# Decoder block on Trainium2: expert biases fetched per tile and added by VectorE, in place of bias products on TensorE

## What is computed

```python
x = _layernorm(x + attn(x, ...))                      # with biases on Q, K, V and O
x = _layernorm(x + (ctx @ Wv) @ Wout + bout)          # what the cross-attention comes to
h  = silu(einsum('nd,edh->neh', xf, up_w) + up_b)     # 8 experts, 256 -> 256
ye = einsum('neh,ehd->ned', h, down_w) + down_b       # 256 -> 256
y  = einsum('ned,ne->nd', ye, comb)                   # best 2 of 8 experts, weights renormalised
x = _layernorm(x + y + shared(x))
```

## Time and profile before

| what | value |
|---|---|
| three runs, us | 479.09, 479.58, 479.75 (median 479.58) |
| profiled execution, us | 479.18 |
| its span, us | 477.3 |
| PE busy | 454.2 us, 95% of the span |
| DVE, ACT, POOL busy | 303.3, 288.8, 189.1 us |
| mean granted TensorE clock | 0.982 of full |

### The profile page before, as it was taken

How to read it: one execution, slowest core, us unless ns; L and a number is a source line. 1 busy time by engine, 2 the same in 40 slices (tenths; PEclk the granted TensorE clock), 3 DMA queues, 4 the chain that set the end, 5 groups by cost and what they waited for, 6 DMA issues and landing times.

```text
span 477.3 us, 11145 instructions
## 1 busy us (share of the span) xinstructions
PE 454.2 (95%) x3613; PEld 397.2 (83%) x3613; DVE 303.3 (64%) x1248; ACT 288.8 (61%) x913; POOL 189.1 (40%) x212
## 2 busy tenths in 40 slices
PE   7998999999999999999999999988999999999982
PEld 6886888988889898898988988877898889999961
DVE  3376598557695585776765769678885543333496
ACT  3686556665666567556675565865534464665556
POOL 1899297220002001211142654434512874655530
PEclk9999899999999999999999999999998999999995
DMA  5851121410010000020011213211021663343775
GB/s 166 304 173 45 60 89 45 135 45 1 1 45 2 1 13 23 24 78 1 1 46 43 83 54 117 62 45 48 33 68 57 177 171 109 113 121 113 226 256 180
DMA packets 26541, 40.28 MB, mean 84 GB/s; under 512 B 3199, under 2 KB 17555, under 8 KB 26483
## 3 DMA queue, kind: packets, MB, share of 16 engines
q1 hardware_dynamic: 21532, 27.86, 19.0%
q0 software_dynamic: 3408, 9.33, 5.4%
q10 hardware_dynamic: 1547, 2.40, 1.7%
HBM read 26.96 MB, written 12.61 MB: 83 GB/s over the span
## 4 chain that ended last, share of the span: by engine, by line
PE 83%; DVE 8%; ACT 5%; DMA 2%; issue 1%; ACTq 0%; SPq 0%; DVEq 0%
PE bank L297 18%; PE bank L298 17%; PE bank L299 17%; PE bank L813 6%; PE bank L775 6%; PE bank L786 6%; PE bank L838 3%; PE bank L953 2%; ACT probs L1114 2%; PE bank L943 2%; PE bank L967 2%; PE bank L861 1%; PE bank L728 1%; DVE xt_lo L1312 1%; DMA xacc<-in_x_t 1%
## 5 line engine op out<-in xcount | busy, mean ns | idle before, releaser
L1114 ACT ACTIVATE probs<-probs,negmax 128x128 f32<-128x128 f32 x256 | 99.7, 394 | 50.6 <-DVE negmax L1341 50.5
L297 PE MATMUL bank<-w_hi,ot_hi 128*128 (+1 forms) x284 | 83.4, 294 | 3.2 <-ACT qkv L1085 3.0
L298 PE MATMUL bank<-w_lo,ot_hi 128*128 (+1 forms) x284 | 81.1, 285 | 0.0
L299 PE MATMUL bank<-w_hi,ot_lo 128*128 (+1 forms) x284 | 80.6, 284 | 0.0
L1341 DVE CUSTOM_DVE_ANT_0 probs<-bank,mask 128x128 f32<-128x128 f32 x256 | 61.1, 284 | 14.2 <-PE bank L775 14.1
L584 POOL DMA_INDIRECT xg_dram<-xacc,place x32 | 32.1, 1005 | 92.7 <-PE bank L813 35.0
L297 PE MATMUL bank<-xt_hi,w_hi 128*128 128x512 f32 x144 | 61.4, 426 | 1.6 <-DVE w_lo L1322 0.6
L297 PEld LDWEIGHTS bank<-w_hi,ot_hi 128*128 128x128 f32 x284 | 54.3, 191 | 6.9 <-ACT qkv L1085 3.8
L1077 ACT ACTIVATE qkv<-bank,cols 128x512 f32<-128x512 f32 x64 | 42.1, 678 | 29.5 <-PE bank L299 29.5
L299 PE MATMUL bank<-xt_hi,w_lo 128*128 128x512 f32 x144 | 56.9, 395 | 0.0
L298 PE MATMUL bank<-xt_lo,w_hi 128*128 128x512 f32 x144 | 56.8, 395 | 0.0
(11 more groups left out here) (215 smaller groups left out, 1036.2 us busy)
## 6 DMA issues: line engine op xcount, KB each, us to landing
qkv<-xg_dram SPq DMA_DIRECT2D x39, 128.5 KB, 2.1
ex_raw<-in_w_experts SPq DMA_DIRECT2D x18, 256.0 KB, 2.6
w_raw<-in_w_quads SPq DMA_DIRECT2D x10, 256.0 KB, 4.7
xacc<-in_x SPq DMA_DIRECT2D x4, 512.0 KB, 3.6
ex_raw<-in_w_cross SPq DMA_DIRECT2D x4, 512.0 KB, 3.2
w_raw<-in_ctx_t_in ACTq DMA_DIRECT2D x4, 512.0 KB, 3.8
w_raw<-in_w_quads SPq DMA_DIRECT2D x3, 512.0 KB, 7.1
xacc<-in_x_t SPq DMA_DIRECT2D x3, 512.0 KB, 6.3
```

What stands on the lines that cost most here:

```text
L297: pe.matmul(o, a_hi, b_hi, start=first, stop=False)
L298: pe.matmul(o, a_hi, b_lo, start=False, stop=False)
L299: return pe.matmul(o, a_lo, b_hi, start=False, stop=last)
L1114: nc.scalar.activation(tile, tile, ACT.Exp, scale=-1.0, bias=negmax[:, s.par, h, j:j + 1], accum_out=sums[:, s.par, h, j:j + 1]).then_inc( ...
```

## The change

The two bias products of a tile go, and so do the nine expert rows of `rows` (only `bout` is left, with one column of `sel`). The down biases, with the shared one added, are written to a small DRAM tensor `down_rows`; the up biases are in `up_rows` as before. For each tile SP reads the expert's number from `list_e` and issues a DMA that copies that bias row to all 128 partitions, once for up and once for down, each into two buffers (`BR`). DVE adds the bias while it evacuates PSUM: `tile_up_bias` writes `th`, on which SiLU then works in SBUF, and `tile_y`, which was ACT's, is DVE's. ACT takes x_hi(i+2) ahead of silu(i). `load_y` of groups 0 to 2 moves from SP to ACT's queue.

```diff
@@ sync
+            def load_bias(i, into, of, landed, taken):
+                if i >= BR:
+                    sp.wait_ge(taken, i - BR + 1)
+                e = sp.value_load(list_e[0:1, i:i + 1], min_val=0, max_val=NE)
+                sp.dma_start(into[:, i % BR, :], of[bass.ds(e, 1), :].rearrange("o n -> (o n)").partition_broadcast(P)
+                             ).then_inc(landed[i % BR], 16)
+            sp.wait_ge(in_down_rows, 16)
+            for i in range(BR):
+                load_bias(i, up_b, up_of, in_up_b, up_added)
+                load_bias(i, down_b, down_rows, in_down_b, yt_ready)
             for g in range(G - 1):
                 sp.wait_ge(sent[g], 16 * 2 * GT)
-            for i in range(TILES):
+            for i in range(TILES + 6):
+                if BR <= i - 4 < TILES:
+                    load_bias(i - 4, up_b, up_of, in_up_b, up_added)
+                if BR <= i - 6 < TILES:
+                    load_bias(i - 6, down_b, down_rows, in_down_b, yt_ready)
+                if i >= TILES:
+                    continue
@@ sync, after the loop
-            for b in range(YR):
-                sp.wait_ge(y_sent[b], 16 * len(range(b, EARLY + MIDDLE, YR)))
-            for g in range(G - 1):
-                load_y(g)
@@ tensor
-                pe.matmul(o, sel[:, 0, :], rows[:, bass.ds(e, 1), :].rearrange("p e n -> p (e n)"),
-                          start=True, stop=False)
...
-                pe.matmul(o, sel[:, 1, :], rows[:, bass.ds(e, 1), :].rearrange("p e n -> p (e n)"),
-                          start=True, stop=False)
@@ scalar
             for i in range(TILES + 2):
+                if i + 2 < TILES:
+                    tile_x_hi(i + 2)
                 if i < TILES:
                     tile_silu(i)
-                if i + 2 < TILES:
-                    tile_x_hi(i + 2)
                 if 0 <= i - 1 < TILES:
                     tile_h_hi(i - 1)
-                if i >= 2:
-                    tile_y(i - 2)
...
+                g = i - (EARLY + MIDDLE + 3)
+                if g == 0:
+                    for b in range(YR):
+                        act.wait_ge(y_sent[b], 16 * len(range(b, EARLY + MIDDLE, YR)))
+                if 0 <= g < G - 1:
+                    load_y(act, g)
@@ vector
+            def tile_up_bias(i):
+                dve.wait_ge(t_up_done, i + 1)
+                dve.wait_ge(in_up_b[i % BR], 16 * (i // BR + 1))
+                if i >= 2:
+                    dve.wait_ge(th_turned, i - 1)
+                nc.vector.tensor_tensor(th[:, i % 2, :], t_up[i % 2][:, 0:D], up_b[:, i % BR, :], ALU.add
+                                        ).then_inc(up_added, 1)
+            def tile_y(i):
+                dve.wait_ge(t_down_done, i + 1)
+                dve.wait_ge(in_down_b[i % BR], 16 * (i // BR + 1))
+                if i >= YR:
+                    dve.wait_ge(y_sent[i % YR], 16 * (i // YR))
+                nc.vector.tensor_tensor(yt[:, i % YR, :], t_down[i % 2][:, 0:D], down_b[:, i % BR, :], ALU.add
+                                        ).then_inc(yt_ready, 1)
@@ vector, the loop: up_bias(i), x_lo(i+2), h_lo(i-1), y(i-2)
```

More of the change, by code:

```diff
@@ L90, in decoder_program @@
         ot_lo = sb("ot_lo", [P, 2, GROUP], F32R)
-        rows = sb("rows", [P, NX + 1, D], F32R)
-        sel = sb("sel", [P, 2, P], F32R)
+        rows = sb("rows", [P, D], F32R)
+        up_b = sb("up_b", [P, BR, D])
+        down_b = sb("down_b", [P, BR, D])
+        sel = sb("sel", [P, P], F32R)
         ex_raw = sb("ex_raw", [P, 2, KT * D])
@@ L261, in decoder_program @@
                                                        sem("cols_taken"))
-        bias_moved = sem("bias_moved")
+        bias_moved, in_down_rows = sem("bias_moved"), sem("in_down_rows")
+        in_up_b = [sem(f"in_up_b{b}") for b in range(BR)]
+        in_down_b = [sem(f"in_down_b{b}") for b in range(BR)]
+        up_added = sem("up_added")
         rows_zeroed, in_up_rows, in_rows, rows_ready = (sem("rows_zeroed"), sem("in_up_rows"), sem("in_rows"),
@@ L334, in after, with load_y @@
             return SPG * g + SPG + 1 + r
+        def load_y(queue, g):
+            src = y_dram[slices(g, 2 * GROUP), :].rearrange("(t p c) d -> c p t d", p=P, c=2)
+            for c in range(2):
+                queue.dma_start(yg[g][c], src[c]).then_inc(in_y[g][c], 16)
         @block.sync
@@ L439, in _ @@
                 sp.dma_start(xg[:, i % XR, :], xg_dram[bass.ds(row, P), :]).then_inc(in_xg[i % XR], 16)
[L441 to L444, removed]
-            for b in range(YR):
-                sp.wait_ge(y_sent[b], 16 * len(range(b, EARLY + MIDDLE, YR)))
-            for g in range(G - 1):
-                load_y(g)
             for b in range(YR):
                 sp.wait_ge(y_sent[b], 16 * len(range(b, TILES, YR)))
-            load_y(G - 1)
+            load_y(sp, G - 1)
             for n, g in enumerate(FINISH[:-1]):
@@ L835, in cross @@
                     o = cross_bank[g][half][:, slices(j, D)]
-                    pe.matmul(o, sel[:, 0, :], rows[:, BOUT, :], start=True, stop=False)
+                    pe.matmul(o, sel[:, :], rows[:, :], start=True, stop=False)
                     for k in range(KT):
@@ L948, in tile_up @@
                 if i >= 2:
-                    pe.wait_ge(th_ready, i - 1)
+                    pe.wait_ge(up_added, i - 1)
                 else:
@@ L1156, in make_sel @@
                 act.wait_ge(sel_col_ready, 1)
-                for half in range(2):
-                    last = nc.scalar.activation(sel[:, half, :], ident[:, :], ACT.Identity, scale=0.0,
-                                                bias=sel_col[:, half:half + 1])
+                last = nc.scalar.activation(sel[:, :], ident[:, :], ACT.Identity, scale=0.0, bias=sel_col[:, :])
                 last.then_inc(sel_ready, 1)
@@ L1200, in tile_silu @@
             def tile_silu(i):
[L1201 to L1204 removed]
+                act.wait_ge(up_added, i + 1)
+                nc.scalar.activation(th[:, i % 2, :], th[:, i % 2, :], ACT.Silu).then_inc(th_ready, 1)
             def tile_h_hi(i):
@@ L1797, in _ @@
             parts = best_two(G - 1)
-            for i in range(TILES + 1):
+            for i in range(TILES + 2):
+                if i < TILES:
+                    tile_up_bias(i)
                 if i + 2 < TILES:
```

63 lines of the change are left out of this document (27 added, 36 removed).

## The result

The changed kernel takes 527.74 us (median of 4 runs, 527.49 to 528.15) against 479.66 us for the kernel before in the same rounds: a ratio of 1.1005 (95% interval 1.0986 to 1.1024), 48 us slower. The span of the profiled execution is 525.9 us.

The account below looks back on a forecast made before the run. SP's queue was to bound the expert stage: 112 loads at 1.12 us plus 1.6 of waits from 358.5, then landing, add and last tile to 491.5, last stage to 512.2, 1 for y's loads, 1.9 around the span: 515 us, range 492 to 530.

Parts of the forecast that it names:

- SP's queue becomes the bound: Expert stage: three loads a tile at 1.12 us make SP need 3.36 us against PE's 2.03; chance 0.60.
- The rule weighed in the prediction: DMA issue on SP: sequencer time is usually small beside the DMA, so SP's three loads would cost nothing.
- Two signs that the forecast named: Expert stage: PE busy some 60%, and DVE's up add waiting for the bias DMA, not for PE.
- SP's chain: Expert stage: 112 loads at 1.12 us, 125.4 us, plus 1.6 of waits from 358.5, last issue ending at 485.5.
- landing rival: Two bias buffers: landings of 8.0 us make 4.6 us a tile, about 550 us in all; chance 0.05.
- 1 us for y's loads: End of the expert stage: y's early groups, 3 MB on ACT's queue, slow the last bias loads by 1 us.
- the worth of the products: PE, 39 tiles: two products of 0.12 us fewer in each save 9.4 us.
- the faster rival: Expert stage: SP keeps up at 0.68 us a load or less, PE stays the bound, 471.5 us; chance 0.10.
- DVE at nothing: DVE in the expert stage: two adds of 0.42 us per tile cost nothing while tiles take more than 2.1 us.
- The 8 us set aside for a loop through DVE and ACT: Up add, SiLU, h_hi, h_lo, y: up to 0.2 us a tile, 8 us, if tiles don't take more than 2.1 us.
- SP cheaper: SP's queue: tracing stretches its steps, a load is 0.85 us, 30 us less, 485 us; chance 0.09 for 484 to 500.
- Low clock: PE in the expert stage: gaps bring the clock to 0.50, 3.5 us a tile, 519.5 us; chance 0.13.

Follow-up runs that it names:

- e4: Kernel before, bias products kept, with the changed kernel's 78 bias transfers and list reads added on SP, unused, and y's early loads on ACT: 525.5 us.
- e9: Kernel before with 78 unused bias transfers of fixed row 0 on SP, without list reads, and y's early loads on ACT: 491.6 us.
- e1: Kernel before without its two bias products per tile and nothing in their place, so without the experts' biases: 477.9 us, ratio 0.9936.
- e2: Changed kernel with every bias transfer copying row 0, so SP reads no list for it; transfers and waits stay: 501.7 us.
- e5: Changed kernel with four buffers for each kind of bias row in place of two: 524.9 us, ratio 1.0901.
- e10: Bias rows resident in SBUF, no bias transfers in the loop, DVE adding a fixed row without a list read: 482.5 us, 1.0050 of the kernel before.
- e8: Bias rows brought into SBUF once, no bias load per tile; DVE reads the list itself and adds: 492.6 us, 1.0212 of the kernel before.
- e6: Changed kernel with fixed row 0 for every bias transfer, no list read for it, and four buffers of each kind: 500.1 us, ratio 1.0420.

## Why the prediction held, and what in it was wrong

**Held: SP's queue becomes the bound.** The forecast gave 1.12 us a load and 3.36 us a tile; the steady tile is 3.51. Between the issue of up bias 2 at 355.08 and that of up bias 38 at 491.75 there are 111 steps, with a median distance of 1.13 us. From 440 to 480 us the chain of work runs through SP's queue alone. e4 shows the same loss with the bias work on PE and DVE unchanged. Splitting it by e9: the transfers, their issues and y's loads on ACT are together 2.4% (12 us, some of it the early stop that e1 has too), the list reads on SP ahead of them another 6.7% (1.0909 - 1.0241; 32 us), and the reads are all in which these two runs differ. The rule weighed in the prediction, that the sequencer's time is small beside the DMA (the Trainium skill, "DMA: Bandwidth & Descriptors", "Issuing engines are not separate DMA queues"), does not fit here: this 32 us is sequencer time. It nearly fits without a read, where a load is 0.47 us of SP (e2).

Two signs that the forecast named came out only in part. PE is busy 74% of 400 to 440 us, not some 60%. And of the 54.8 us for which DVE stood idle before the up adds, the profile puts 10.5 down to the landing of the bias, 15.7 to PE and 28.0 to nothing that it shows. The bias is late all the same: in tiles 17 to 30 the add starts 2.9 to 4.9 us, in the median 3.5, after the issue of its own bias.

**In the range, by errors that partly cancel: SP's chain.** The forecast had the last up bias start at 485.2; it started 6.6 us later. Its start was 3.4 us too late (first add at 358.5, where SP issued up bias 2 at 355.08; the first add was at 353.9), and the length was 10 us too short: 111 steps at 1.12 us are 124 us, and measured are 136.7. The chain was not "without a pause". The largest pause, 361.40 to 366.00, is a tile load waiting for POOL's target row behind POOL's scatters; SP's waits from 356 to 492 us (waited for, us in total, times, longest) have others for the adds, the two-buffer wait that the forecast named in its landing rival but put at nothing in the sum:

```profile
SPq L438 <- DVE qkv L1723: 2.0, 3, 1.4
SPq L438 <- DVE qkv L1715: 1.9, 3, 0.8
```

In all 28 of the 111 steps are over 1.3 us long; they hold 15 us more than at 1.12 us each. About half of that is neither the pause nor these waits, and stays unexplained. That the early start made up for a third of it was luck.

**Wrong: the end, 1 us for y's loads, and nothing for the two buffers.** From the start of the last bias issue to the end of its add the forecast had 2.5 us; measured are 7.6 (491.75 to 499.38). The early groups of y, 3 MB, were issued from 483.5 to 491.0, and their landing took up to 9.2 us; the DMA share from 480 to 505 is 0.74 and the granted clock 0.74. The down biases of the last tiles then waited for their buffers, 8.2 us in four waits, one of 3.7, and the last was added at 504.79. This is the loop of the forecast's landing rival, which the sum left out: from 482 to 506 us 61% of the chain is the landing of three down biases (start, us).

```profile
483.76 5.65 DMA down_b<-down_rows
...
490.71 6.05 DMA down_b<-down_rows
...
501.80 2.91 DMA down_b<-down_rows
```

Between them stand an add on DVE and the read and issue on SP, 0.8 us. The add of the last up bias comes at 498.96 because DVE first waited, until 496.84, for the down bias of tile 35, and then worked on the expert sums until 499.04. So it is not that add's own bias that was seen to be late. e5, with four buffers, sends its last y 3.4 us earlier, 1.9 of them gained after tile 30. Along the forecast's own path the error adds up as follows. From the end of the last up add to DVE's last stage the forecast had 3.8 us, measured are 5.8. So the last stage began 13.6 us later than forecast: 6.6 on SP, 5.1 from the last issue to its add, 2.0 behind it; with the 1 us set aside that is the 12.7 us by which the forecast was low. The length of the last stage was right: 20.8 us against 20.7.

**Wrong: the worth of the products.** The forecast took 2 x 0.12 us a tile and 9.4 us in all. e1 gives 0.17 us a tile and 3.1 us in all. It did not reach the forecast's time, since PE was not the bound any more, but it bears on the faster rival: with SP free the time would not have been 471.5 (e10, with the adds and SP free, is 482.5).

**Half right: DVE at nothing.** In steady tiles the adds cost nothing (e10). What the forecast missed are the tiles in which DVE has other work too, up to 4.8 us (e10 against e1 at the last y, part of it at half clock). The 8 us set aside for a loop through DVE and ACT were not seen: the 8 us that e8 loses against e10 come from the list read behind the wait, which the changed kernel does not have on DVE.

**The rivals.** SP cheaper, or PE still the bound: ruled out by the steps of 1.1 us and by e4. Low clock: the granted clock fell to 0.50 in eight stretches from 369.2 us on, the first of 3.4 us and the longest of some 10; but up to 480 us these are 20 us in all, the mean is 0.96 from 400 to 440 and 0.91 from 440 to 480, and in the latter the chain is SP's alone, so the low clock is not on it there. It lasts only at the end. Landing over 5 us: seen on the chain only at the end, 5.7 and 6.1 us.

**Open.** e2 and e6 have 2.74 and 2.76 us a steady tile. Adds without transfers give 2.15 (e10), transfers without adds 2.40 (e9); the two together cost some 0.35 us more than the longer of the two, and four buffers don't change it. In e6 SP waited from 400 to 450 us for POOL's target rows, 9.0 us in 12 waits, and the chain ends on POOL and can't be followed past it; the loop through the tile load, PE, DVE's y, POOL's scatter and target and SP is the likely place, but this is argued, not shown. Nor was y's load alone moved to see what of the end is its doing.

## What to carry to other kernels

Price a transfer with a run-time address by what its queue does before it, too: the register read, the check and the address. Here these were 0.65 of 1.12 us, and three such loads a tile made an idle queue the bound. Count the steps of the issuing queue per iteration before work is moved off an engine; a queue of which the page shows no busy time can be the fullest one. A value read behind a wait is on the path of what the wait releases, on VectorE as on SP. With few buffers the landing is part of the price too, once it stands in a loop of wait, issue, landing and use. And removing two products of 0.12 us from a full PE gave 0.17 us, not 0.24, since the gap between tiles grew from 0.20 to 0.28.

## What was not expected of the hardware

- A broadcast load of 128 KB keeps SP for 0.47 us with a fixed row and for 1.12 us with a row from a list: the read (0.27 us) is less than half of the difference.
- VectorE's own read of a list took 0.305 us and the register step behind it 0.19 us; together 1.6% of the time, 8 us, over 39 tiles (e8 against e10).
- Doubling the DMA share of the steady tiles (0.38 to 0.78, e9) lengthened them by 0.10 us only.
- Without the bias products tiles 0 to 9 take 29.2 us (e1) against 24.4 before: a start 3.5 us earlier, a stop of PE of 3.9 us and then 6.8 us at a granted clock of 0.50 which the kernel before did not have. e9, with work added, shows the same stop and fall, so that leaving work out is their cause is not shown.
